# Four-layer graph network on one core: ScalarE issues all loads of destination rows, behind its rectifier

## What is computed

```python
# layer 0 ("mlp")
x = concatenate([node_feats[src], node_feats[dst], edge_feats], axis=1)
m = maximum(x @ W1 + b1, 0.0) @ W2 + b2
out = segment_sum(m, dst)
# layer 1 ("gatv"), 4 heads of 16
g = leaky_relu(xl[src] + xr[dst] + edge_attr @ W_e, 0.2)
logits = einsum('ehc,hc->eh', g, att)
alpha = softmax of logits over the edges of one dst
out = segment_sum(xl[src] * alpha, dst)      # then batch norm and GELU
```

## Time and profile before

| | us |
|---|---|
| median of 3 runs | 6524.55 (6518.11 to 6526.9) |
| the profiled execution | 6519.98 |
| its span in the trace | 6518.3 |

### The profile page before, as it was taken

The page is one execution under the profiler, slowest core; times in us unless marked ns, Lnnn a source line. Parts: engine busy times, 40 slices in busy tenths (PEclk is TensorE's granted clock), DMA queues, the critical chain, the costliest instruction groups (busy, mean ns, idle before and its releaser), DMA issues. The chain is left out here.

```text
span 6518.3 us, 104392 instructions
## 1 busy us (share of the span) xinstructions
PE 4711.5 (72%) x33332; PEld 3513.2 (54%) x33332; DVE 3868.5 (59%) x7682; ACT 1957.4 (30%) x4434; POOL 4020.3 (62%) x4127
## 2 busy tenths in 40 slices
PE   4476777777777774577777777777776379999689
PEld 3455666666666654455665565556655232222189
DVE  3122555555555532466666666666655469999855
ACT  1111222222222211222222222222211159999710
POOL 5666566666666665366666666666666537777634
PEclk7555565565656555555555555555555579999899
DMA  7754455555555543344444444444444234444298
GB/s 182 129 139 131 139 154 148 148 147 147 152 151 154 152 116 86 82 129 132 131 132 131 130 131 131 130 123 130 130 134 113 60 113 129 126 128 126 74 337 300
DMA packets 891151, 905.22 MB, mean 139 GB/s; under 512 B 629433, under 2 KB 773203, under 8 KB 874480
## 3 DMA queue, kind: packets, MB, share of 16 engines
q1 hardware_dynamic: 562512, 710.78, 35.2%
q0 software_dynamic: 115488, 115.45, 9.2%
q10 hardware_dynamic: 212608, 72.31, 4.7%
HBM read 659.37 MB, written 239.54 MB: 138 GB/s over the span
## 5 line engine op out<-in xcount | busy, mean ns | idle before, releaser
L515 POOL DMA_INDIRECT gatv_G<-gatv_src,src_cols x1612 | 1529.7, 949 | 944.0 <-DMA work<-in_x_turned 440.1
L515 POOL DMA_INDIRECT mlp_G<-mlp_src,src_cols x1612 | 1531.9, 950 | 924.0 <-issue 427.6
L706 DVE TENSOR_TENSOR mlp_hots<-mlp_in_psum,src_lo 128x1024 bf16<-128x1024 bf16 x608 | 417.2, 686 | 701.8 <-remote 639.2
L929 PE MATMUL mlp_sums<-mlp_zs,mlp_same 128*128 128x64 f32 x3234 | 735.6, 413 | 92.6 <-issue 83.0
L929 PE MATMUL gatv_sums<-gatv_msg,gatv_same 128*128 128x68 f32 x3234 | 707.9, 402 | 102.0 <-issue 100.9
L893 PE MATMUL mlp_z<-mlp_win,mlp_hot 128*128 128x64 bf16 x4851 | 432.5, 233 | 478.8 <-issue 478.0
L929 PEld LDWEIGHTS gatv_sums<-gatv_msg,gatv_same 128*128 128x128 f32 x3234 | 692.7, 318 | 140.3 <-issue 140.1
L929 PEld LDWEIGHTS mlp_sums<-mlp_zs,mlp_same 128*128 128x128 f32 x3234 | 697.5, 322 | 100.5 <-issue 99.1
L893 PEld LDWEIGHTS mlp_z<-mlp_win,mlp_hot 128*128 128x128 bf16 x4851 | 357.1, 127 | 645.1 <-issue 619.9
L2292 POOL TENSOR_TENSOR keys<-src_lo,gsoft_ring 128x512 f32<-128x512 f32 (+1 forms) x448 | 504.7, 1132 | 186.7 <-ACT src_lo L2434 177.9
L2357 PE MATMUL gsoft_acc<-keys,masks 128*64 128x512 f32 (+1 forms) x1568 | 558.8, 621 | 78.2 <-DVE keys L2530 43.0
(11 more groups left out here) (504 smaller groups left out, 8216.0 us busy)
## 6 DMA issues: line engine op xcount, KB each, us to landing
mean_block<-blocks SPq DMA_DIRECT2D x61, 1568.0 KB
gsoft_ring<-blocks SPq DMA_DIRECT2D x105, 896.0 KB
sums_gatv<-gatv_out_rows SPq DMA_DIRECT2D x231, 252.0 KB
mlp_rel<-rel_rows SPq DMA_DIRECT2D x116, 448.0 KB
gatv_rel<-rel_rows SPq DMA_DIRECT2D x116, 448.0 KB
sums_mlp<-mlp_out_rows SPq DMA_DIRECT2D x231, 224.0 KB
blocks<-masks SPq DMA_DIRECT2D x31, 1568.0 KB
blocks<-work SPq DMA_DIRECT2D x31, 1568.0 KB
```

The costliest lines, as they stand in the source:

```text
L515: pool.indirect_dma_start(out=G[:, b.gq, j * L.gathered:(j + 1) * L.gathered], out_offset=None, in_=L.gather_table, in_offset=bass.Indirec ...
L706: last = nc.vector.tensor_tensor(hot_of[:, slot(b, k), :, :, :], bc(steps2_of[:, 0:w, :], 1, [P, OCTET // K2, w, K2]), bc(of_step[:, cols] ...
L929: last = pe.matmul(sums[:, j * L.msg:(j + 1) * L.msg], same[:, b.q, j, :], rhs, start=True, stop=True)
```

## The change

SyncE issues no loads of windows any more. ScalarE issues all seven of batch i+2 in its step i, with the same wait as before, but behind `nonlinear(i)` and not at the step's start. In the first pass the copy of octet (i-2, 3), in the second the exponentials and the sums' copy, now come ahead of them; the other octet copies, and in the first pass the sums' copy, come behind them.

```diff
-SP_TILES = 4
@@ edge_pass, sync, step(i), for batch b = i + 2
-                        load_windows(nc, sp, L, S, win, win_in, b, range(0, SP_TILES))
@@ edge_pass, scalar
             def step(i):
-                w = i + 2
-                if L.window and w.exists():
-                    wait(act, z_made, w.used(Q))
-                    load_windows(nc, act, L, S, win, win_in, w, range(SP_TILES, B))
                 p, d = i + (-1), i + (-2)
                 if not soft and d.exists() and builds(d):
                     copy_octet(d, per_batch - 1)
...
                 if L.window and i.exists():
                     nonlinear(i)
+                w = i + 2
+                if L.window and w.exists():
+                    wait(act, z_made, w.used(Q))
+                    load_windows(nc, act, L, S, win, win_in, w, range(B))
                 if soft and d.exists() and builds(d):
                     copy_octet(d, per_batch - 1)
                 if p.exists() and builds(p):
```

## The result

Before 6519.9 us (6510.3 to 6526.9), after **6559.2 us** (6549.5 to 6564.7), medians of 5 runs each; the ratio is 1.0058, 95% interval 1.0047 to 1.0070. So the change costs 39 us. I had predicted slower, by 104 us. The profiled spans are 6518.3 and 6551.8, 33.5 us apart; it is this difference that the traces can be asked about.

What follows compares the result with a forecast made beforehand. TensorE's z, finished just past the end of the gathers' drain, was taken to set the building stage's pace. The sum 6519.98 + 114 - 10 = 6624, with 4.6 added for the median, gave 6629 us; range 6495 to 6790.

Steps and rivals of the forecast that it cites:

- Step 6: Building stage of the first pass: z 2.45 us late lengthens each batch by 0.75 us, 114 us over 152 batches.
- the term for the cover: Building stage: 1.0 us taken off z's 2.45 us delay, because the start of TensorE's slow matmuls moves with z.
- the formula: Building stage: each batch grows by z's delay less the cover, halved, (2.45 - 1.0) / 2 = 0.75 us.
- the halving: Building stage: GpSimd's later restart moves TensorE's slow stretch along, so half of z's delay reaches the period, d = m/2.
- the trickle absorbs it: Building stage: late z runs full pace into TensorE's slow time; within 0.08 us a batch, 6512 to 6538 us; chance 0.2.
- my likeliest rival: Building stage: windows late, z without slack, 0.2 to 1.5 us a batch, 6550 to 6750 us; chance 0.45.
- Step 1: SyncE loses four loads, 3.93 us per batch; its other work moves forward, nothing gained: 0 us.
- Step 7: First pass's other 79 batches: windows also late, but TensorE is about one z ahead; 0 us, at most 24.
- Step 2: ScalarE loses three loads at its step's front: nothing in the building stage, 10 us gained in the second pass.
- Step 3: ScalarE's seven loads behind its rectifier can begin some 0.8 us behind it and take 3.15 us.
- Step 4: Building stage: octet copies queue behind ScalarE's loads, so TensorE reaches z about 1.2 us late; the smaller overlapping delay.
- Step 5: Building stage: windows land 2.6 us after their last issue, so z starts 2.45 us later; the larger overlapping delay.

Runs made afterwards that it cites:

- the start kept: The changed kernel, but with before's order in steps 0 to 11 of the first pass and ahead of them: 1.0030 of before, +20 us.

## Why the prediction was wrong in size

**Step 6 failed, by the term for the cover.** It let z lose 2.45 us and took off 1.0 us, from how the trickle's start moved between two batches. The delay itself was right in size, 2.35 us in the median, but by luck: it comes from the copies, which I had at 1.2 us, and not from the windows. The cover is 3.2 us: the whole of the trickle, not only the move of its start. A late z sends its matmuls at full pace into time in which they crept before. With 3.2 in place of 1.0 the formula gives (2.45 - 3.2) / 2, nothing, where 9 us were measured over 144 batches. It also gives (5.12 - 3.2) / 2 = 0.96 us for the kernel with seven idle activations and the loads, where 0.72 was measured. That doesn't show the halving, by which GpSimd's restart carries the trickle along: it is one kernel, and in the pair with four gathers, which has no trickle to hide in, z starts 4.1 us later behind the rectifier (7.04 against 2.96 in the median) for 1.0 us of period, a quarter of it. My rival "the trickle absorbs it" had the mechanism. I gave it 0.2 because I read the earlier trace rows as a law for the trickle's start when they were one batch of another stage. Its price, 6512 to 6538 us, still missed, as it holds no early loss. And that 6559 lies in the range of my likeliest rival (6550 to 6750) is luck: that range stood for 0.2 to 1.5 us a batch, and 0.06 were measured.

Step 1, SyncE's loads at no price and no gain, was wrong: taking them off SyncE costs ScalarE 14 loads in a row at the start, 4.7 us at once, and shifts SyncE's big store out of the long stop. I had asked what SyncE's other work gains by coming earlier, and not what it meets there. With the start kept the change costs 20 us instead of 39. Step 7 had covered these batches with one term for late windows in a steady state, at most 24 us for "the other 79 batches"; in the traces those stretches cost 5.2 + 14.2 + 3.0 + 4.1 = 26.5 us, and what of it is explained has other reasons, a start-up row and a store.

Step 2, 10 us gained in the second pass, didn't come: 2396.9 us against 2396.5, and the run that keeps before's order there is no slower than the whole change. GpSimd's mean pause in that pass stayed at 1.98 us against 1.99. The drain of seven gathers binds, as the earlier trace rows had suggested.

Step 3 was right in the size of the loads (3.31 us for seven, 3.15 predicted), but they begin 2.15 us behind the rectifier in that batch, 1.42 in the median, not 0.8: three loads begin 0.57 us behind it, seven 1.42, so by my estimate each further row number costs ScalarE about 0.2 us ahead of the first load, (1.42 - 0.57) / 4.

Steps 4 and 5 were exchanged in weight. Step 4, the octet's copy, binds (2.41 us of TensorE's wait in the rows above), and z starts at R+7.6 because the copies come a microsecond later than I had them. Step 5 was too dear: the windows were there 1.7 us behind their last issue at the latest (1929.73 to 1931.44), and 1.5 us in the kernel with the loads behind the copies, not 2.6. The Trainium skill (DMA: Bandwidth & Descriptors, "Anatomy of one DMA") has about 2.0 us as a small transfer's fixed time, fitted for GpSimd's path; these rows show less than that behind the end of the issue row, and were nearer to it than my 2.6. With 2.0 in place of 2.6 my own formula falls by 30 us, not by the some 40 that I wrote.

The other page that I had weighed holds at the start: by the Trainium skill (DMA: Bandwidth & Descriptors, "Issuing engines are not separate DMA queues") a second issuing engine saves time on the issuing engine only. The trace agrees, with 13.21 us for 14 loads in one row against 6.73 and 7.54 us side by side, and there that time was on the path.

**What stays open.** The 0.06 to 0.09 us a batch of the building stage. It comes with z hardly late in two kernels, three loads or seven idle activations behind the rectifier, so it isn't the price of z's delay; the octet copies are late in all of them. Seven loads in front of it cost 0.05 us too. Fourteen idle activations put copy and z where the change has them and cost 0.21 us, three times as much, so the copies' delay alone doesn't explain it either. And the 7 to 12 us between batch 200 and the second pass I only located: no run took them apart, and kernels with before's order there differ among themselves by up to 8 us.

## What to carry to other kernels

Where instructions creep because another engine's transfers drain, a delay ahead of them is nearly free up to the whole time that they creep (0.06 to 0.21 us a batch here for delays of up to 2.35 us), so measure that time (here z to sums, 6.50 against a floor of 3.27) before charging a delay, and charge only what exceeds it. Look at the start-up by itself when loads move between issuing engines: one long row of first loads, and a big store that leaves the gap in which it was hidden, cost more here than 152 batches of a later z. A place that is harmless for three loads can be wrong for seven, and a place further back that frees one wait can bring up the next: behind the copies the same loads cost twice as much.

## What the hardware showed that I had not expected

Cutting the gathers to four a batch cut the period from some 10.6 to 7.6 us and took the trickle away with it, so TensorE's slow pace inside z (one matmul per 0.7 us) belongs to the drain and not to TensorE's own work. In the long stop at 155 to 215 us, where six batches of gathers drain, most matmuls came one per 1.5 to 3.5 us, and in the kernel after ScalarE stood idle for 56.48 us ahead of one copy, with only the issue of seven loads in between. The chips differed by 1.2% in this kernel's drain-bound second pass, 10.43 us a batch on one and 10.56 on another, with the same program.
